# Splitting a reciprocal square root into two halves and moving four transposes behind one matmul

## The reference

```python
def layernorm(x, scale, bias):
    m = mean(x); v = mean(square(x - m))
    return (x - m) * rsqrt(v + 1e-6) * scale + bias

def block(x):                      # eight times, x is (8, 256, 128)
    q, k, v = x @ Wq + bq, x @ Wk + bk, x @ Wv + bv
    Q, K = elu(q) + 1, elu(k) + 1
    KV, Ksum = sum_s(K * v), sum_s(K)
    V = Q * KV / (Q * Ksum + 1e-6)
    x = layernorm(gelu(V @ Wo + bo) + x, ln1_s, ln1_b)      # the first norm
    h = gelu(x @ Wf1 + bf1)                                 # 128 -> 512
    return layernorm(gelu(h @ Wf2 + bf2) + x, ln2_s, ln2_b) # the last norm
```

## Time and profile before

| | us |
|---|---|
| median of 3 runs | 525.33 |
| the three runs | 526.71, 525.21, 525.33 |
| time of the profiled execution | 526.34 |
| span in its profile | 524.1 |

### The profile page before, as it was taken

How to read it: one execution, slowest core, us unless ns; L and a number is a source line. 1 busy time by engine, 2 the same in 40 slices (tenths; PEclk the granted TensorE clock), 3 DMA queues, 4 the chain that set the end, 5 groups by cost and what they waited for, 6 DMA issues and landing times.

```text
span 524.1 us, 8271 instructions
## 1 busy us (share of the span) xinstructions
PE 504.4 (96%) x1996; PEld 309.3 (59%) x1996; DVE 429.8 (82%) x1633; ACT 405.2 (77%) x603; POOL 294.6 (56%) x327
## 2 busy tenths in 40 slices
PE   7789999999999999999999999999989899899997
PEld 5345565555555555655555555556546477677785
DVE  5889888988898888889888988888887667777754
ACT  4758888888888888888888888888889666657452
POOL 4435655566565666555665656655556376555552
PEclk9989999999999999999999999999999999999999
DMA  8200010001000000100010000001000000000000
GB/s 249 88 16 1 7 41 15 0 5 40 15 5 20 20 15 5 40 15 0 5 40 15 5 20 20 15 5 40 1 0 1 2 0 1 21 1 21 2 21 20
DMA packets 16070, 11.22 MB, mean 21 GB/s; under 512 B 8220, under 2 KB 13852, under 8 KB 16052
## 3 DMA queue, kind: packets, MB, share of 16 engines
q1 hardware_dynamic: 15188, 10.29, 7.1%
q10 hardware_dynamic: 864, 0.73, 0.4%
HBM read 9.96 MB, written 1.05 MB: 21 GB/s over the span
## 4 chain that ended last, share of the span: by engine, by line
PE 82%; DVE 8%; issue 3%; POOL 3%; ACT 2%; DMA 1%; DVEq 0%; POOLq 0%; ACTq 0%
PE bank L436 20%; PE bank L427 15%; PE bank L302 12%; PE bank L448 6%; PE bank L424 5%; PE bank L344 4%; PE bank L349 4%; PE bank L345 4%; PE bank L544 2%; PE bank L546 2%; PE bank L545 2%; PE bank L604 1%; DVE sc L1327 1%; PE bank L589 1%; PE bank L590 1%
## 5 line engine op out<-in xcount | busy, mean ns | idle before, releaser
L436 PE MATMUL bank<-hid,wf 128*128 128x512 f32 x256 | 120.2, 592 | 0.0
L913 POOL TENSOR_TENSOR rsD<-veD,c_half 128x4 f32<-128x4 f32 x32 | 37.3, 1166 | 102.1 <-DVE veD L1025 102.1
L427 PE MATMUL bank<-x,wf 128*128 128x512 f32 x192 | 93.6, 597 | 0.0
L751 ACT ACTIVATE hid<-bank,vbf 128x512 f32<-128x512 f32 x128 | 77.6, 694 | 0.2 <-PE bank L427 0.2
L436 PEld LDWEIGHTS bank<-hid,wf 128*128 128x128 f32 x256 | 46.1, 190 | 46.5 <-issue 31.1
L996 POOL TENSOR_TENSOR xs_lo<-sc,xs_hi 128x512 fp32r<-128x512 f32 x36 | 46.7, 1296 | 45.3 <-ACT xs_hi L869 44.0
L427 PEld LDWEIGHTS bank<-x,wf 128*128 128x128 f32 x192 | 35.3, 191 | 33.4 <-issue 16.3
L1115 DVE TENSOR_SCALAR x<-bank,vln 128x256 f32<-128x256 f32 x64 | 31.9, 540 | 23.8 <-PE bank L302 23.8
L1044 DVE TENSOR_SCALAR xhB<-bank,meanB,rsB 128x128 f32<-128x128 f32 x128 | 43.7, 404 | 8.8 <-POOL rsB L913 8.8
L721 ACT ACTIVATE g<-bank,vbf 128x512 f32<-128x512 f32 x31 | 21.4, 691 | 35.6 <-PE bank L436 35.6
L1044 DVE TENSOR_SCALAR xhD<-bank,meanD,rsD 128x128 f32<-128x128 f32 x128 | 43.7, 404 | 5.0 <-POOL rsD L913 0.7
(11 more groups left out here) (178 smaller groups left out, 1181.2 us busy)
## 6 DMA issues: line engine op xcount, KB each, us to landing
wf<-in_w_f SPq DMA_DIRECT2D x16, 256.0 KB, 2.6
wu<-in_w_unit SPq DMA_DIRECT2D x10, 192.0 KB
wqkv<-in_w_qkv SPq DMA_DIRECT2D x7, 192.0 KB, 2.3
x<-in_x SPq DMA_DIRECT2D x4, 256.0 KB, 5.2
out<-ot SPq DMA_DIRECT2D x3, 256.0 KB, 2.2
wo<-in_w_o SPq DMA_DIRECT2D x8, 64.0 KB, 1.8
wmod<-in_w_mod ACTq DMA_DIRECT2D x1, 256.0 KB, 5.4
vln<-in_v_ln SPq DMA_DIRECT2D x16, 1.0 KB, 1.7
```

What stands on the lines that cost most here:

```text
L427: mm = nc.tensor.matmul(ps_ff[j][:], wf1[:, j * P:(j + 1) * P], x2[(c - 2) % CH][:], start=True, stop=True)
L436: mm = nc.tensor.matmul(ps_f0[:], wf2[:, j, :], hid[:, j, :], start=(j == 0), stop=(j == FJ - 1))
L751: nc.scalar.activation(hid[:, j, :], ps_ff[j][:], ACT.Gelu_apprx_tanh, bias=vbf1[:, j:j + 1]).then_inc(h_ready, 1)
L913: nc.gpsimd.tensor_tensor(rs[buf(k, n)][:], ve[buf(k, n)][:], c_half[:], ALU.pow).then_inc(rstd_ready[k], 1)
```

## The change

Two edits, both within a round.

1. The power of the first norm (tag "B" in `rstd`, POOL) is issued as two instructions on two columns each (128x2) in place of one on four (128x4), and each signals on its own. In `normalize` (DVE) the first tile waits for the first signal and the third tile for the second; before, the first tile waited for the one signal. The norms "I", "D" and "F" keep one power.
2. On PE the low product of v stands directly behind those of k and q, and the transposes of `y2` behind it.

```diff
@@ PE, slot
+                if has(a) and not plain(a):
+                    qkv_low("v", ps_v).then_inc(v_mm, 1)
                 if has(d) and has(b):
                     last_norm_to_tm()
-                if has(a) and not plain(a):
-                    qkv_low("v", ps_v).then_inc(v_mm, 1)
@@ POOL, rstd
                 pool.wait_ge(var_ready[k], n + 1)
+                if k == "B":
+                    for h in range(HB):
+                        part = slice(h * T // 2, (h + 1) * T // 2)
+                        nc.gpsimd.tensor_tensor(rs[k][:, part], ve[k][:, part], c_half[:, part],
+                                                ALU.pow).then_inc(rstd_ready[k], 1)
+                    return
@@ DVE, normalize
-                dve.wait_ge(rstd_ready[k], n + 1)
                 for j in range(T):
+                    if k == "B" and j % (T // 2) == 0:
+                        dve.wait_ge(rstd_ready[k], HB * n + j // (T // 2) + 1)
+                    elif k != "B" and j == 0:
+                        dve.wait_ge(rstd_ready[k], n + 1)
```

## The result

| | us |
|---|---|
| before, median | 525.33 |
| changed, median | 527.46 (527.14 to 528.44) |
| ratio | 1.0036, 95% interval 1.0025 to 1.0048 |
| forecast | 525.2, range 523.2 to 529.6 |

The change makes the kernel slower by 2.1 us. The time lies in the range, but I forecast no change, and the interval of the ratio excludes one.

The account below looks back on a forecast made before the run. The prediction took the ring through ACT (`dd`, then `vt`) to bound the kernel. Its terms, +0.35 in the loop, -0.2 ahead and -0.15 behind, gave 0.0, with -0.1 for roundings: 525.2 us against 525.33, range 523.2 to 529.6.

Parts of the forecast that it names:

- the two waits of 8.8 and 8.7 us: DVE waits 8.8 us in 25 rounds for `rsB`, PE's weight loader 8.7 us in 28 rounds for `y2`.
- the ring through ACT: Path from `g2` through `dd`, `vt`, output product, `y1` transposes to next `g2`; claimed without slack, nearly the whole round.
- the sum of 11.95: Stretches from one `g2` to the next, 4.77 + 3.53 + 3.65 us, set beside a round of 12.07.
- PE is the bound after all: Rival: each round saves 0.30 us on PE, 8.4 over 28 rounds, giving 516.9 us; chance 0.04.
- rounds fall to their bare sum: Rival: ACT's ring isn't rigid; four rounds save up to 0.2 us, giving 523.6 us; chance 0.09.
- Part one, worth of the early half: DVE's 0.33 us wait for `rsB` goes; `xhB` transposes start 0.08 earlier; worth 0 us in a loop round.
- Part one, cost of the pair: Two half powers of 0.6 us occupy POOL 0.2 longer ahead of `y2`; bounds 0 and 1.0.
- this rival: POOL's pair costs too much, delaying `vt`; 529.6 us at 0.4 extra; chance 0.16 for 526.9 to 529.6, 0.08 beyond.
- The tens of cycles: Skill's call cost on POOL: the pair well under 0.1 us more, the kernel's sum 0.4 us lower.
- Part two, new order: Low product of v ahead of `y2` transposes on PE: first round of a layer loses 0.05 to 0.17 us.
- The gain of 0.05: Second round: `vt` 0.05 us late against up to 0.1 won by PE being ready for the output product.
- The sum: Loop +0.05 us a layer, +0.35 in seven passes; ahead of the loop -0.2, behind it -0.15; in all 0.0.

Follow-up runs that it names:

- dd_first: The kernel before with one exchange on ACT, `dd` computed ahead of `ek`: 522.43 us, ratio 0.9951.
- quarters: The changed kernel with four powers of one column, each with its own signal and wait, in place of two of two: 549.95 us, ratio 1.0468.
- order_not_first: The kernel before with PE's new order in three rounds of four, the first round of each layer keeping the old order; one power: 525.47 us, ratio 1.0002.
- order_only: The kernel before with PE's new order alone, one power of four columns: 526.32 us, ratio 1.0023.
- order_pad2: The kernel before with PE's new order, one power, and a 128x2 addition on unused tiles behind it on POOL: 525.99 us, ratio 1.0016.
- order_pad72: The kernel before with PE's new order, one power, and a 128x72 addition on unused tiles behind it on POOL: 526.99 us, ratio 1.0035.

## Why the prediction was wrong, point by point

**What bounds the kernel** was read rightly. The share of 96% for PE and the two waits of 8.8 and 8.7 us both pointed at the wrong thing, and so does the chain that ended last (82% PE, 2% ACT); the ring through ACT was the one: `dd_first` shows it. What carried the reading was `vt` 0.10 and 0.11 behind `dd`, not the sum of 11.95. That sum adds up the stretches from one `g2` to the next, and comes out as the distance between them whatever lies in between; the 12.07 beside it was measured from product to product and reaches into the next round. So the 0.12 between the two is no sign of time that could be won. The rivals "PE is the bound after all" and "rounds fall to their bare sum" are out.

**Part one, worth of the early half:** 0 in the loop, as forecast. The 0.33 wait went, and the normalized chunk waited for PE instead (the transposes of `xhB` at 232.44 follow the high products without a wait).

**Part one, cost of the pair:** this is the step that failed. I wrote "I take 0.2, by the nearest row", and the nearest row was an addition on a 128x2 tile, 0.197 us. What an instruction pays whatever it holds was read from another operation, as if any instruction on POOL paid the same. It is 0.39 for a power, and the pair costs 0.35 more than the one, not 0.2. I gave the point from which this rival decides as 0.3, and the pair lies beyond it; both signs that I named for it came, a half above 0.65 and `vt` behind `stD` and no longer behind `dd`. With 0.35 in the prediction's own sum: the pair delays `vt` by 0.35 less the slack of 0.15 in the second round, which is 0.20, and by 0.35 less 0.29, which is 0.06, in the fourth; measured 0.16 and 0.04. With about 0.13 for the third, between them, and 0.1 to 0.15 in the first, that is some 0.5 a layer, 3.6 us, less 0.35 ahead of and behind the loop: about 528.6. The right mechanism with the right price would still have been 1.1 too high against the 527.46 measured. Most of that is the third round, which lost only 0.02: the statistics started 0.75 behind the transposes there before and 0.69 after, so they came 0.29 late and not 0.35, against a slack of 0.25 (`vt` 1.06 behind the statistics before, 0.81 when it has to wait for them).

**The tens of cycles** that the Trainium skill gives for an instruction's call on POOL (GPSIMD Engine Reference, Instruction dispatch) would have been still further off for this operation: `quarters` shows 0.39 us of fixed cost for a power. What of it is the call and what the power's own start, no run here parts.

**Part two, new order:** forecast 0.05 to 0.17 in the first round of a layer, 0.10 taken; measured 0.13, and gone in `order_not_first`. The gain of 0.05 that I put against it in the second round didn't come (12.05 in both): the product started 0.85 behind `vt` before and 0.86 with the new order, however early PE was ready.

**The sum** was +0.35 for the loop and is +2.5. Ahead of the loop I forecast 0.2 and the change won about 0.3: the second `g2` of the profile comes at 49.80 in the changed kernel and at 50.10 in `order_only`. Behind the loop I forecast 0.15, and about 0.1 came: the last three distances from `g2` to `g2` sum to 34.69 in the changed kernel and to 34.79 before.

**The chances:** 0.24 for slower, of which 0.16 lay between 526.9 and 529.6. Both ends of the unknown cost stood in the text; between 0 and 1.0 I took a value 0.1 below the deciding point and gave it 0.63.

## What to carry to other kernels

Before an instruction is split so that its first half comes early, find what stands behind it on its own engine and how much slack that has: here the split released a wait that nobody needed and lengthened a queue that somebody did. A fixed cost read from one operation is no price for another on the same engine; if the deciding point lies close to the estimate, measure the split instruction by itself. And in a pipeline whose rounds are a ring of hand-overs, ask of each consumer how long it starts behind each of its producers: in this kernel the one with 0.1 in every round was the one to move, and that took an exchange of two activations, not a cure for the two waits that the change aimed at.

## What the runs showed of the hardware

The power `rsB` on POOL takes 0.549, 0.709 and 1.02 us for one, two and four columns on 128 partitions (`quarters`, changed, before): 0.39 and 0.16 a column. An addition of two columns takes 0.197. I had not expected the operation itself to have the larger fixed part. The price isn't the same everywhere, though: the power of the last norm, of the same shape, takes 1.17 in the kernel before:

```profile
L913 POOL TENSOR_TENSOR rsD<-veD,c_half 128x4 f32<-128x4 f32 x32 | 37.3, 1166 | 102.1 <-DVE veD L1025 102.1
```

What the other engines do at that time differs, and no run parts the cause.

A small instruction can cost its queue less than its row shows: the 128x2 addition, 0.19 us long, kept the next instruction's start back by 0.15 in three rounds of four (`order_pad2`), and the 128x72 one, 0.30 long, by 0.26 (`order_pad72`).
